# Bias rows and a sum row added by three-row bf16 matmuls in place of one-row fp32 matmuls

## What is computed

```python
# layer 0, feed-forward: logits of 64 slices for each of 8 heads
x_mid = (x @ W_x + b_x).reshape(B, N, H, D).transpose(0, 2, 1, 3)
slice_weights = softmax((x_mid @ W_slice + b_slice) / temp, axis=-1)

# layer 1, mixing (beside the relational sum over edges)
qkv = (x @ Wqkv.T + bqkv).reshape(B, N, 3, H, D)
vsum = jnp.sum(vN, axis=-2)[:, :, None, :]
y = A * einsum(qn, qn, kv_mod) + scale**2 * Bc * einsum(qn, kv) + scale**4 * Cc * vsum
out = jnp.transpose(y / y_norm, (0, 2, 1, 3)).reshape(B, N, H * D)
return out @ Wproj.T + bproj
```

## Time and profile before

| | |
|---|---|
| median of three runs | 7969.41 us (7962.21 to 7973.39) |
| span of the profiled execution | 7942.4 us, 87092 instructions |
| median less span (work around the span) | 27.0 us |
| mean granted clock of PE | 0.841 |

### The profile page before, as it was taken

One profiled execution on the slowest core, in us unless ns is written; L12 is line 12 of the kernel. 1 busy time (PEld: TensorE's weight loads), 2 busy tenths in 40 slices (PEclk: granted clock), 3 DMA queues, 4 the chain that ended last, 5 costly groups with the idle time before them and its releaser, 6 DMA issues. The chain is left out here.

```text
span 7942.4 us, 87092 instructions
## 1 busy us (share of the span) xinstructions
PE 5581.7 (70%) x25066; PEld 3810.3 (48%) x25066; DVE 5151.1 (65%) x11656; ACT 1874.7 (24%) x4564; POOL 3471.0 (44%) x3440
## 2 busy tenths in 40 slices
PE   5877773555555655528799788887999999960991
PEld 2446652333333433314454334443777777750661
DVE  6467777888888877764367566666666666660332
ACT  0333332222223332212134200000222222220220
POOL 0000005777777777700000455555666667625006
PEclk8998886677777777759899899998998999965995
DMA  4100004444555555510013322222333333332223
GB/s 145 42 26 1 1 1 105 124 123 124 125 127 130 134 130 129 126 38 0 17 78 132 112 68 70 71 72 72 89 95 87 89 95 95 92 77 80 63 64 107
DMA packets 310174, 665.89 MB, mean 84 GB/s; under 512 B 77964, under 2 KB 173950, under 8 KB 302701
## 3 DMA queue, kind: packets, MB, share of 16 engines
q0 software_dynamic: 180352, 455.22, 22.7%
q1 hardware_dynamic: 129367, 205.30, 7.5%
HBM read 546.51 MB, written 113.55 MB: 83 GB/s over the span
## 5 line engine op out<-in xcount | busy, mean ns | idle before, releaser
L2026 POOL DMA_INDIRECT ag_rows<-table,row_src x1612 | 1594.9, 989 | 2007.2 <-POOLq L2813 1052.5
L1123 POOL DMA_INDIRECT at_rows<-table,row_dst x1612 | 1633.9, 1014 | 491.0 <-issue 448.9
L1289 PE MATMUL at_p_a<-at_rows,at_hot 128*125 128x264 f32 x3224 | 1137.0, 511 | 997.3 <-issue 976.8
L1289 PEld LDWEIGHTS at_p_a<-at_rows,at_hot 128*125 128x125 f32 x3224 | 708.6, 246 | 1184.9 <-issue 1045.2
L1252 DVE TENSOR_TENSOR acc<-acc,at_p_a 125x264 f32 x1612 | 687.4, 426 | 244.3 <-PE at_p_a L1289 101.4
L2388 PE MATMUL mo_p_e<-ag_rows,ag_hot 128*125 128x256 f32 x2192 | 651.0, 422 | 265.0 <-DVE acc L2232 231.5
L2232 DVE TENSOR_TENSOR acc<-acc,mo_p_e 125x256 f32 x1096 | 459.3, 419 | 498.7 <-PE mo_p_e L2388 308.0
L2388 PEld LDWEIGHTS mo_p_e<-ag_rows,ag_hot 128*125 128x125 f32 x2192 | 392.0, 199 | 480.3 <-DVE acc L2232 376.3
L2136 DVE TENSOR_TENSOR mo_prod<-mo_far,mo_twice 125x256 f32<-125x256 f32 x1600 | 580.1, 419 | 50.9 <-issue 44.3
L1075 POOL PARTITION_ALL_REDUCE sb_top<-sb_top x1 | 0.4, 397 | 1220.5 <-DVE sb_top L1046 1220.5
L1239 DVE TENSOR_TENSOR at_rows<-at_rows 128x1024 f32<-128x1024 f32 x496 | 496.9, 1022 | 21.8 <-ACT at_rows L1171 21.5
(11 more groups left out here) (475 smaller groups left out, 9944.2 us busy)
## 6 DMA issues: line engine op xcount, KB each, us to landing
at_wide<-node_t SPq DMA_DIRECT2D x124, 406.2 KB
table<-rt_row SPq DMA_DIRECT2D x50, 1000.0 KB
at_rows<-table,row_dst POOLq DMA_INDIRECT x1612
ag_rows<-table,row_src POOLq DMA_INDIRECT x1612, 2.8
moe_in<-ones SPq DMA_DIRECT2D x1, 13440.0 KB
ex_space<-moe_in SPq DMA_DIRECT2D x105, 128.0 KB, 2.2
moe_out<-ex_space SPq DMA_DIRECT2D x105, 128.0 KB, 1.7
table<-row SPq DMA_DIRECT2D x50, 128.9 KB
```

The lines of the kernel that those rows point to most:

```text
L1123: pool.indirect_dma_start(out=rows[n % 3][:, g, :], out_offset=None, in_=m.table0, in_offset=bass.IndirectOffsetOnAxis(ap=row_i[:, n * G + ...
L1289: pe.matmul(p_a[k % BANKS][0:P, 0:TW], hot[n % 2][:, g, :], rows[n % 3][:, g, :], start=True, stop=True).then_inc(s_agg, 1)
L2026: pool.indirect_dma_start(out=rows[:, i % RING, j, :], out_offset=None, in_=m.table1, in_offset=bass.IndirectOffsetOnAxis(ap=row_i[:, 2 * ...
```

## The change

A row of fp32 is split into three bf16 rows whose sum is the fp32 row: its rounding to bf16, the rounding of what is left, and that of what is left then. The three rows lie on three partitions, and a matmul with three rows of bf16 ones (`m.ones3`) adds them up in the fp32 accumulator. The helper `three_terms` works on three equal copies of the row, one on each partition, and uses columns of the identity matrix to keep only the k-th term on partition k. It is called at three places on DVE: on `b_log` (512 columns) at the end of `slice_logits_weights`; on all four biases of the mixing step together (1024 columns) before `weave`; and on `v_sum` (264 columns) at the turn. The copies come from DMAs that broadcast to three partitions, from a `b_x` tile repeated in three columns, and from three columns of ones in the sum over nodes. All biases of the mixing step are now loaded at the start, before the wait, and a new semaphore `s_bias` holds PE's first bias matmul until the terms are there.

```diff
+    m.ones3 = sb("ones3", [3, 128], BF16)
...
+def three_terms(dve, m, row, rest, term, out):
+    dve.tensor_copy(term, row)
+    dve.drain()
+    dve.tensor_scalar(out, term, m.ident[0:3, 0:1], None, ALU.mult)
+    dve.tensor_tensor(rest, row, term, ALU.subtract)
+    dve.drain()
+    for k in (1, 2):
+        dve.tensor_copy(term, rest)
+        dve.drain()
+        dve.scalar_tensor_tensor(out=out, in0=term, scalar=m.ident[0:3, k:k + 1], in1=out, op0=ALU.mult, op1=ALU.add)
+        if k == 1:
+            dve.tensor_tensor(rest, rest, term, ALU.subtract)
+        dve.drain()
...
+                dve.tensor_copy(b_x[:, :, :], b_x1[:, :].unsqueeze(2).broadcast_to((128, 4, 3)))
...
-                b = b_log[0:1, :].rearrange("p (h g) -> p h g", h=H)
-                dve.tensor_tensor(b, p_b[0:1, :].rearrange("p (h g) -> p h g", h=H),
-                                  b_s[0:1, :].unsqueeze(1).broadcast_to((1, H, SL)), ALU.add)
+                b = b_all[:, :].rearrange("p (h g) -> p h g", h=H)
+                dve.tensor_tensor(b, p_b[0:3, :].rearrange("p (h g) -> p h g", h=H),
+                                  b_s[:, :].unsqueeze(1).broadcast_to((3, H, SL)), ALU.add)
                 dve.drain()
-                dve.tensor_tensor(b, b, temp[0:1, :].unsqueeze(2).broadcast_to((1, H, SL)), ALU.mult)
+                dve.tensor_tensor(b, b, temp[0:3, :].unsqueeze(2).broadcast_to((3, H, SL)), ALU.mult)
+                dve.drain()
+                three_terms(dve, m, b_all[:, :], b_rest[:, :], b_term[:, :], b_log[:, :])
...
-                    mm = pe.matmul(p_b[0:1, 128 * o:128 * o + 128], b_x[:, o:o + 1], two[:, :], start=True, stop=True)
+                    mm = pe.matmul(p_b[0:3, 128 * o:128 * o + 128], b_x[:, o, :], two[:, :], start=True, stop=True)
...
-                    pe.matmul(p_l[u][0:P, :], m.ones[0:1, 0:P], b_log[0:1, :], start=False, stop=True).then_inc(s_log, 1)
+                    pe.matmul(p_l[u][0:P, :], m.ones3[:, 0:P], b_log[:, :], start=False, stop=True).then_inc(s_log, 1)
...
+        b_in, b_rest = (prod[1][0:3, k:k + 2, :, :].rearrange("p h s i -> p (h s i)") for k in (0, 2))
+        b_term = prod[1][0:3, 4, :, :].rearrange("p s i -> p (s i)").bitcast(BF16)
+        v_in, v_rest, v_term = (prod[1][0:3, k, :, :].rearrange("p s i -> p (s i)") for k in (1, 3, 5))
+        v_in, v_rest, v_term = v_in[:, 0:2 * HALF], v_rest[:, 0:2 * HALF], v_term.bitcast(BF16)[:, 0:2 * HALF]
...
-                sp.dma_start(b[:, :], a["L1_mix_bqkv"][C:3 * C].rearrange("(o n) -> o n", o=1)).then_inc(s_w, 16)
+                for lo, bias in ((0, a["L1_mix_bqkv"][C:3 * C]), (2 * C, a["L1_mix_bqkv"][0:C]), (3 * C, a["L1_mix_bproj"])):
+                    wide = bias.rearrange("(o n) -> o n", o=1)
+                    sp.dma_start(b_in[:, lo:lo + wide.shape[1]], wide.broadcast_to((3, wide.shape[1]))).then_inc(s_w, 16)
                 sp.dma_start(temp[:, :], a["L1_mix_temperature"].rearrange("a h b c -> a (h b c)").broadcast_to((P, H))).then_inc(s_w, 16)
-                sp.wait_ge(s_w, 48)
+                sp.wait_ge(s_w, 80)
                 sp.wait_ge(s_kv, NT)
                 sp.dma_start(w_q, a["L1_mix_Wqkv"][:, 0:C].rearrange("(c p) n -> p c n", p=128)).then_inc(s_w, 16)
-                sp.dma_start(b_q, a["L1_mix_bqkv"][0:C].rearrange("(o n) -> o n", o=1)).then_inc(s_w, 16)
                 sp.dma_start(w_p, a["L1_mix_Wproj"].rearrange("(c p) n -> p c n", p=128)).then_inc(s_w, 16)
-                sp.dma_start(b_p, a["L1_mix_bproj"].rearrange("(o n) -> o n", o=1)).then_inc(s_w, 16)
...
-                                        dve.tensor_scalar(v_sum[0:1, g, :], p_one(g), Q_SCALE ** 4 / N, None, ALU.mult)
+                                        dve.tensor_scalar(v_in[:, HALF * g:HALF * g + HALF], p_one(g), Q_SCALE ** 4 / N, None,
+                                                          ALU.mult)
                                     dve.drain()
+                                    three_terms(dve, m, v_in, v_rest, v_term, v_sum[:, :, :].rearrange("p g v -> p (g v)"))
...
-                dve.wait_ge(s_w, 48)
+                dve.wait_ge(s_w, 80)
                 dve.tensor_scalar(temp[:, :], temp[:, :], Q_SCALE ** 2, None, ALU.mult)
-                dve.drain()
+                three_terms(dve, m, b_in, b_rest, b_term, b3[:, :])
+                dve.drain().then_inc(s_bias, 1)
...
-                        return add(p_one(g), m.ones[0:P, 0:1], half)
+                        return add(p_one(g), m.ones[0:P, 0:3], half)
...
+                                    if k == 0:
+                                        pe.wait_ge(s_bias, 1)
                                     for out, lo in ((p_k, 0), (p_v, C)):
                                         for c in range(2):
                                             pe.matmul(out, xt[:, c, :], w[:, c, lo:lo + C], start=c == 0, stop=False)
-                                        mm = pe.matmul(out, m.ones[0:1, 0:P], b[0:1, lo:lo + C], start=False, stop=True)
+                                        mm = pe.matmul(out, m.ones3[:, 0:P], b3[:, lo:lo + C], start=False, stop=True)
...
-                                    pe.matmul(p_q, m.ones[0:1, 0:P], b_q[0:1, :], start=False, stop=True).then_inc(r_q, 1)
+                                    pe.matmul(p_q, m.ones3[:, 0:P], b3[:, 2 * C:3 * C], start=False, stop=True).then_inc(r_q, 1)
...
-                                    pe.matmul(p_y[n % 2][0:P, 0:2 * HALF], m.ones[0:1, 0:P],
-                                              v_sum[0:1, :, :].rearrange("p g v -> p (g v)"),
+                                    pe.matmul(p_y[n % 2][0:P, 0:2 * HALF], m.ones3[:, 0:P],
+                                              v_sum[:, :, :].rearrange("p g v -> p (g v)"),
...
-                                    pe.matmul(p_o[0:P, 256:512], m.ones[0:1, 0:P], b_p[0:1, :], start=False, stop=True
+                                    pe.matmul(p_o[0:P, 256:512], m.ones3[:, 0:P], b3[:, 3 * C:4 * C], start=False, stop=True
```

More of the change, by code:

```diff
@@ L90, in _ @@
             pool.memset(m.ones[:, :], 1.0).then_inc(m.s_const, 1)
+            pool.memset(m.ones3[:, :], 1.0)
             pool.iota(m.count_p[:, :], [[1, P]], base=0, channel_multiplier=0,
@@ L1385, in slice_logits_weights @@
         two = sb("sw_two", [128, 128], F32)
-        b_x = sb("sw_b_x", [128, 4], F32)
-        b_s = sb("sw_b_s", [1, SL], F32)
+        b_x1 = sb("sw_b_x1", [128, 4], F32)
+        b_x = sb("sw_b_x", [128, 4, 3], F32)
+        b_s = sb("sw_b_s", [3, SL], F32)
+        b_all = sb("sw_b_all", [3, H * SL], F32)
+        b_rest = sb("sw_b_rest", [3, H * SL], F32)
+        b_term = sb("sw_b_term", [3, H * SL], BF16)
         temp = sb("sw_temp", [128, H], F32)
@@ L1396, in _ @@
                 sp.dma_start(w_x[:, :, :], a["L0_ffn_W_x"].rearrange("(c p) n -> p c n", p=128)).then_inc(s_w, 16)
-                sp.dma_start(b_x[:, :], a["L0_ffn_b_x"].rearrange("(o p) -> p o", p=128), allow_slow_non_contiguous=True).then_inc(s_w, 16)
-                sp.dma_start(b_s[:, :], a["L0_ffn_b_slice"].rearrange("(o p) -> o p", o=1)).then_inc(s_w, 16)
+                sp.dma_start(b_x1[:, :], a["L0_ffn_b_x"].rearrange("(o p) -> p o", p=128), allow_slow_non_contiguous=True).then_inc(s_w, 16)
+                sp.dma_start(b_s[:, :], a["L0_ffn_b_slice"].rearrange("(o p) -> o p", o=1).broadcast_to((3, SL))).then_inc(s_w, 16)
                 sp.dma_start(temp[:, :], a["L0_ffn_temperature"].rearrange("a h b c -> a (h b c)").broadcast_to((128, H))).then_inc(s_w, 16)
@@ L1988, in relational_mix @@
         m_far = sb("m_far", [128, 2, 2, HALF], F32)
-        v_sum = sb("v_sum", [1, 2, HALF], F32)
+        v_sum = sb("v_sum", [3, 2, HALF], BF16)
         part = [sb(f"qa_part{k}", [128, 4, P], F32) for k in range(2)]
@@ L2004, in relational_mix @@
         p_lin = lambda g: p_m[1][:, HALF * g:HALF * g + HALF]
-        p_one = lambda g: p_m[g][0:1, 2 * HALF:3 * HALF]
+        p_one = lambda g: p_m[g][0:3, 2 * HALF:3 * HALF]
         p_c = p_n[0:2]
@@ L2009, in relational_mix @@
         heads = lambda x: x.rearrange("p (h f) -> p h f", h=H)
-        s_w, s_zero, s_near, s_back, s_moved = (sem("mo_" + x) for x in ("s_w", "s_zero", "s_near", "s_back", "s_moved"))
+        s_w, s_zero, s_near, s_back, s_moved, s_bias = (sem("mo_" + x) for x in ("s_w", "s_zero", "s_near", "s_back", "s_moved", "s_bias"))
         s_xn, s_tr, s_xt, s_kv, s_sq, s_sum, s_root, s_v, s_k, s_prod, s_fold = (sem("mo_" + x) for x in (
@@ L2391, in edge_work @@
                         yield
-                pe.wait_ge(s_w, 48)
+                pe.wait_ge(s_w, 80)
                 pe.wait_ge(s_zero, 1)
@@ L2874, in program @@
                             w_log = logits.enter_context(nc.sbuf_tensor("w_log", [128, 2, H * SL], F32))
-                            b_log = logits.enter_context(nc.sbuf_tensor("b_log", [1, H * SL], F32))
+                            b_log = logits.enter_context(nc.sbuf_tensor("b_log", [3, H * SL], BF16))
```

3 lines of the change are left out of this document (1 added, 2 removed).

## The result

The changed kernel takes 7847.89 us (median of 4 runs, 7844.48 to 7856.85) against 7971.40 us (median of 4, 7962.21 to 7975.79): ratio 0.9849, 95% interval 0.9835 to 0.9863, 123.5 us less. The forecast was 7882 us.

What follows compares the result with a forecast made beforehand. No engine is full; PE leads the relational stage's second half, a ring of dependent work paces slice tiles. 32.5 + 27 + 40 - 12 = 87.5 us gained, 7969.4 to 7882 us; range 7845 to 7935.

Steps and rivals of the forecast that it cites:

- The 27 us "outside the span": Whole kernel: 27 us between the profiled span (7942.4 us) and the median (7969.4 us) lie outside the span and don't change.
- The fixed part of a slot: Replaced matmuls on PE: the part of each slot independent of columns stays at 0.19 us, saving 0.32 or 0.65 us.
- the 16 us that would have hung on the shorter one: Relational stage: sum some 16 us larger if the bf16 weight load took L1273's 99 ns.
- The slice stage: 50 matmuls of 512 columns in `slice_weights`: 0.65 us saved each, 32.5 us, all on the path.
- The first half: Relational stage, k and v, 100 matmuls of 256 columns: 33.6 us saved, exposure 0.8, 27 us gained.
- The start: `three_terms` on 1024 columns ahead of the edge work: 8.1 us, DVE's 3.31 us idle covers part, 4.8 us remain.
- The turn: `three_terms` on 264 columns between the relational halves: some 3.4 us, 0.90 us covered, 2.5 us added.
- The second half: Relational stage, `v_sum`, q and projection, 150 matmuls: 50.4 us saved, exposure 0.8, 40 us gained.
- Rival 1: Relational stage: DVE sets the pace and gain is mostly given back; a quarter of 84 us passes, 7928 us; chance 0.18.
- Rival 2: Replaced matmuls: the slot doesn't shrink, only the 12 us added remain, 7981 us; chance 0.06.
- Rival 3: Relational stage: PE's granted clock falls and the kernel is slower, 8008 us at a fall of 0.06; chance 0.06.
- a clock that moved: Both relational halves: the clock stays within 0.02; the prediction is wrong if it moved.

Runs made afterwards that it cites:

- the two padded kernels: Kernel before with fp32 rows, and changed kernel with bf16 rows, each zero-padded to 128 partitions: ratios 0.9857 and 0.9812 against the kernel before.
- early terms: Changed kernel with the 1024-column job moved into DVE's idle time in `slice_logits_weights`, terms loaded from DRAM: 7824.97 us, ratio 0.9842 against the kernel before.
- both padded in bf16: Changed kernel with bf16 rows zero-padded to 128 partitions, without and with the bias terms worked out early: 7804.84 and 7781.43 us.

## Why the prediction was right, and where it was not

The direction, the mechanism and the order of the terms held: the slots shrink, the stages shorten by about their number times the saving, and the clock of both halves stays within 0.02. What it named at its end is seen: a tile period of 6.5 us, the load of L1567 just behind `sl_w`, a slot of 0.25 us. The time came out 34 us under the forecast and 3 us above the low end of its range (7845), and one of the four timed runs (7844.48) lies below that end. Between the two traces the gain was 94.4 us where the sum has 87.5, and that nearness is in part luck: the stages came to +32.4 (slice), -4.7 (its job), +35.4, +55.8, -10.4 and -0.5, of which some 17 are clock; another -11.4 us lie ahead of all the changed places, in the attention stage, and -2.2 between and behind the stages, and no term of the sum was for either. Slots and exposure were off in opposite directions. Step by step:

- **The 27 us "outside the span": wrong.** The profiled execution of the changed kernel has a span of 7848.0 and a time of 7849.75 us: 1.75 us lie outside. In before the span was 7942.4 and the median 7969.41, so the remaining 25.3 us were inside the timed executions: they were slower ones than the profiled. The step that failed is that I took one profiled execution for the typical one and called the difference a constant. Of the 34 us, 25.3 are this, 6.9 the larger gain between the traces (94.4, not 87.5), and 1.9 that the changed kernel's profiled execution was itself a little over its median.
- **The fixed part of a slot: mis-sized.** I kept 0.19 us. It was 0.14 for 256 columns (0.25 - 0.11). The 0.38 us for 512 columns give 0.17 at most, as `sl_w` ended last there. The price a column, 0.413 ns, was right: padded, k's slot is 0.11 and nothing else. So the saving was 0.37 to 0.38 for 256 columns, where the sum has 0.32. The reason given, that the switch of rows stays, is shown right by the two padded kernels; what I missed is that the switch could be taken away, and has another 0.09 us in front. The load measured 128 ns, not the 99 of L1273, so the 16 us that would have hung on the shorter one weren't there.
- **The slice stage: right.** -32.4 us, forecast 32.5. The job on 512 columns took 4.7 us, forecast 4.6. In timed runs this part was worth less, 6 and 18 us by the medians, 14 and 20 by the ratios, and 19 as what the relational part leaves of the whole. The attention stage ahead of it, which ended up to 14 us later in the traces with it, is in the timed numbers; whether by chance or by the change is open.
- **The first half: exposure too low.** 35.4 us, forecast 27. Of 100 x 0.37 x 1.05 = 39 us nine tenths came through, not eight. The matmuls' removal brought about half of what left PE, at a lower clock.
- **The start: the cover was no cover.** +10.4 us, forecast +4.8. The job's length was right (7.7, forecast 8.1). The 3.31 us that DVE "waited for PE" were also the time in which it loads the tile numbers, and the trace names only the later of two. The earlier trace rows showed 2.56 us of the same loading, named "issue", and I used it in another step, but not here. Once DVE came later, the loading stood in full behind the job. PE then waited 8.71 us, and its next four matmuls took 2.07 us, as against 1.13 at full clock.
- **The turn: smaller.** The job took 3.2 us (forecast 3.4), and the stretch grew by 0.5 us, not 2.5. The edge sum behind it had no idle time left.
- **The second half: right by slots, with a clock on top.** -55.8 us, forecast 40. By the windows from 5560 to 6900 us the clock went from 0.94 to 0.96, to four places from 0.9414 to 0.9554. What 0.01 is worth can be estimated from kernels whose slots there are alike: 1498.7 us at 0.9137, 1473.4 at 0.9350 and 1465.8 at 0.9414 (the slice part alone, twice, and before), and 1433.3 at 0.9364 (one bf16 row) against 1410.0 at 0.9554 and 1403.3 at 0.9605 (the change): some 12 us. So of the 55.8 us some 17 are clock and 39 are slots, against 150 x 0.37 x 1.05 = 58: exposure 0.67. The prediction's 40 was reached with a slot saving too small and an exposure too large. Nor is 0.67 a constant of this half: the same reckoning gives 0.7 for the bf16 rows padded to 128 (1398.2 us), but all of the 34 us of slots for the fp32 ones (1409.5 us), and why is open. The reading behind the 0.8 was loose too: the 28 waits of the earlier trace rows are two for every three of the 44 frames of that window, not one a frame.
- **Rival 1** (the gain given back) fell: the two halves are 91.2 us shorter, of the 97 that 39 and 58 us of slots would make with nothing given back, and even without the 17 us of the clock that is 74, far above the 21 of that rival. Its mechanism is there, though, in the waits that shift to DVE. **Rival 2** fell with the slots. **Rival 3** came out with the other sign. Leaving the fourth chip out, the three second halves of the old code are at 0.94, 0.91 and 0.94; with short slots there are six at 0.96 (the change twice, the relational part twice, fp32 padded, early terms), two at 0.95 (both padded in bf16) and two at 0.94 (no bias matmuls, one row). On average this is 0.02 higher. The last of the prediction's own signs of being wrong, a clock that moved, is thus half met: by 0.014 and 0.019 in the two traces of the change, inside the 0.02 that it allowed, but worth 17 us and more. The higher clock of the short slots, on average, can explain why the timed gains (107 to 124 us) stand above the 94.4 of the traces: of the old code's three second halves, that in the trace of before is the shortest. The second trace of before, meant to settle this, did not. That the short slots themselves lift the clock is likely but not shown; the two cases at 0.94 speak against a firm rule.

The clock in the second half, windows from 5560 to 6900 us of the change and of its second trace:

```profile
5560.00:6900.00 1340.00, 1225.28 (x7880) 1066.09 (x7879) 929.63 (x2506) 335.32 (x669) 953.02 (x973) 0.96 0.35 96
```

```profile
5560.00:6900.00 1340.00, 1224.28 (x7918) 1064.85 (x7918) 932.75 (x2515) 337.32 (x673) 957.03 (x979) 0.96 0.35 96
```

## What to carry to other kernels

A small matmul among large ones pays for its few rows on both sides; put the row at the top of a tile of zeros as high as its neighbours before you change its type, and look whether the neighbour behind has few weight columns, as then a part of the cost stays. Measure such a slot from the start of the matmul ahead of it, not from its own load. An idle time whose releaser is another engine may hide that the waiting engine was busy with its own instruction stream, so it is cover only where a neighbouring frame shows that nothing else is in it. And compare a profiled execution with timed ones before you carry the difference over as a constant.

## What the runs showed of the hardware that I had not expected

- A bias matmul of one or three rows between matmuls of 128 costs 0.09 us in front and 0.14 to 0.20 us behind, as much as 140 to 170 columns of fp32, and it holds back the next weight load; with 128 rows both are gone and only the columns remain. A stationary tile of one or three columns behind it keeps some 0.1 us of that, while 125 rows beside 128 cost nothing.
- The number of rows in itself is free: one row and three, and 128 rows by the load of 0.13 and 0.14 us.
- The same program's second half took 1473.4 and 1498.7 us at clocks of 0.94 and 0.91, and its timed runs spread from 7908.85 to 7967.81 us, wider than the gain of its edit.
- One of the four chips of the experiments ran the unchanged kernel 7% longer, 8517.71 us against 7947.77 to 7960.24, with most of it in the attention stage (its end 330 us later) and in the second half at a clock of 0.88, and nothing in the slice stage (361.5 against 360.8 us).
